# Storing in-place halves as they land, one half by plain copy and GpSimd add, and turns ahead of control and sums

## The reference

```python
g = group_norm(x, groups=32)                     # mean and variance of 16 channels x 3136 pixels
r = relu(g)
r = where(max_pixels(r) - mean_pixels(r) < 0.5, 0, r)        # per channel
bb = 1 - exp(-abs(max_channels(r) - mean_channels(r)))       # per pixel
y = bb * r
pooled = mean_pixels(y)
control = sigmoid(pooled @ W1.T) * where(relu(pooled @ W3.T) < 1, 1.2, relu(pooled @ W3.T))
out = x + where(y < control * max_pixels(y), 0, y)
```

## Time and profile before

| | |
|---|---|
| time, median of 3 runs | 1783.85 us (1779.1 to 1792.09) |
| time of the profiled execution | 1780.24 us |
| its span | 1778.4 us |
| granted PE clock, mean | 0.843 |
| DVE busy | 1460.9 us (82%) |
| ACT busy | 1306.6 us (73%) |
| PE busy, matmul records | 1303.4 us (73%), 19616 |
| PEld busy, records | 1080.2 us (61%), 19616 |
| POOL busy | 610.6 us (34%) |
| HBM read, written | 310.38 MB, 205.52 MB |
| DMA plain queue | 416.38 MB, 58.4% of 16 engines |
| DMA accumulating queue | 99.56 MB, 28.7% of 16 engines |

### The profile page before, as it was taken

How to read it: one execution, slowest core, us unless ns; L and a number is a source line. 1 busy time by engine, 2 the same in 40 slices (tenths; PEclk the granted TensorE clock), 3 DMA queues, 4 the chain that set the end, 5 groups by cost and what they waited for, 6 DMA issues and landing times.

```text
span 1778.4 us, 45243 instructions
## 1 busy us (share of the span) xinstructions
PE 1303.4 (73%) x19616; PEld 1080.2 (61%) x19616; DVE 1460.9 (82%) x2192; ACT 1306.6 (73%) x1921; POOL 610.6 (34%) x446
## 2 busy tenths in 40 slices
PE   4888776788876778767688777678777688777761
PEld 3766655666665666655576655566655566656660
DVE  2588887988887988888888887888887887888987
ACT  5678777777787878777767787777787767777821
POOL 0043233443233444223443233443233442233430
PEclk8898888998888898888888888898878887888885
DMA  9259989999999899998989999989999988899973
GB/s 396 87 162 301 319 315 320 281 296 297 312 330 336 277 285 306 302 329 320 287 263 296 307 330 332 283 277 296 301 330 329 279 265 269 315 329 343 296 228 145
DMA packets 93418, 518.86 MB, mean 292 GB/s; under 512 B 10272, under 2 KB 10272, under 8 KB 93216
## 3 DMA queue, kind: packets, MB, share of 16 engines
q1 hardware_dynamic: 75360, 416.38, 58.4%
q0 software_dynamic: 17856, 99.56, 28.7%
HBM read 310.38 MB, written 205.52 MB: 290 GB/s over the span
## 4 chain that ended last, share of the span: by engine, by line
PE 29%; POOL 26%; ACT 22%; DVE 15%; issue 7%; DMA 1%; SPq 0%; DVEq 0%; ACTq 0%; POOLq 0%
POOL xs L778 23%; ACT rs L476 8%; PE ps_turn L286 7%; PE ps_gate L347 7%; ACT xs L476 7%; PE ps_gate L322 6%; PE ps_gate L294 6%; DVE xs L670 6%; ACT rs L451 5%; DVE rs L670 4%; DVE max_and_mean L622 2%; POOL rstd L757 2%; DMA xs<-in_x 1%; PE ps_gate L356 1%; DVE xs L737 1%
## 5 line engine op out<-in xcount | busy, mean ns | idle before, releaser
L622 DVE TENSOR_REDUCE max_and_mean<-ps_turn 128x2 f32<-128x1024 f32 x384 | 466.0, 1220 | 201.3 <-PE ps_turn L286 200.6
L286 PE MATMUL ps_turn<-ident,xs 128*128 128x128 f32 (+1 forms) x1600 | 358.8, 310 | 177.7 <-DVE max_and_mean L622 112.3
L769 POOL DMA_DIRECT2D xs<-in_x x124 | 111.6, 968 | 940.0 <-DVE xs L670 837.0
L778 POOL TENSOR_TENSOR xs<-xs,rs 128x1568 f32<-128x1568 f32 x124 | 433.3, 3531 | 1.9 <-DVE rs L670 1.9
L286 PEld LDWEIGHTS ps_turn<-ident,xs 128*128 128x128 f32 (+1 forms) x1600 | 204.5, 153 | 311.5 <-DVE max_and_mean L622 155.2
L312 PE MATMUL ps_gate<-ident,bb 128*128 128x128 f32 (+1 forms) x1600 | 273.4, 333 | 153.2 <-ACT bb L469 144.0
L425 ACT ACTIVATE scratch<-xs 128x3136 bf16<-128x3136 f32 x128 | 360.2, 2814 | 7.8 <-DMA xs<-in_x 2.8
L312 PEld LDWEIGHTS ps_gate<-ident,bb 128*128 128x128 f32 (+1 forms) x1600 | 249.6, 239 | 173.4 <-DVE ymax_parts L639 157.7
L286 PE MATMUL ps_turn<-ident,rs 128*128 128x128 f32 (+1 forms) x1600 | 341.3, 299 | 6.0 <-issue 6.0
L639 DVE CUSTOM_DVE_ANT_0 xs<-xs,ps_gate 128x768 f32<-128x768 f32 (+1 forms) x256 | 243.3, 959 | 45.1 <-PE ps_gate L312 45.0
L451 ACT ACTIVATE xs<-xs,shift,rstd 128x3136 f32<-128x3136 f32 x64 | 191.9, 2999 | 100.0 <-POOL shift L761 93.3
(11 more groups left out here) (80 smaller groups left out, 991.9 us busy)
## 6 DMA issues: line engine op xcount, KB each, us to landing
xs<-in_x SPq DMA_DIRECT2D x260, 784.0 KB, 13.7
out<-xs SPq DMA_DIRECT2D x256, 784.0 KB, 8.2
xs<-in_x POOLq DMA_DIRECT2D x124, 784.0 KB, 11.1
rs<-in_L_conv_W SPq DMA_DIRECT2D x2, 1024.0 KB, 18.7
```

Of the source, the lines that this page charges most:

```text
L286: mm = pe.transpose(ps_turn[0:w, n % 2, b - 2 * i, P * t:P * (t + 1)], r_tile(s, t)[:, P * b:P * b + w], ident[:, :])
L622: ins = dve.tensor_reduce(max_and_mean[:, 2 * i:2 * i + 2, 0], ps_turn[:, n % 2, :, :], AX.X, ALU.max)
L778: pool.tensor_tensor(o, o, half(r_tile(s - 1, t), h), ALU.add).then_inc(added, 1)
```

## The change

- SP's order within a round: the stores of tile 0 come first, tile 3's and tile 2's follow as their adds end, and each reload stands closer to the store that it waits for. `LOAD_ORDER`, the order in which loads, squares and sums of x take the tiles, becomes 0, 2, 3, 1.
- Half 0 of tile 1 (`AGAIN`) gets its x otherwise: SP copies it from HBM into `scratch`, once the row means of sample `s + 2` and the logits of sample `s` are made (ACT and PE are done with `scratch`), and POOL adds it as a fifth add. ACT's copy of control rows waits for that add. Three accumulating DMAs a sample remain of four.
- PE: turns 1 and 2 run ahead of all control products, which were interleaved with them; turns 3 and 4 run ahead of the sums of x instead of behind them. The group mean square is two accumulating matmuls instead of one, since the first tile's squares now come as two halves.
- ACT: the first tile of squares is split; its first half stands between the copy of the control rows and the exponential. `copy_group` moves ahead of `gate_values(s, 0)`, and a second `pool_sum` ahead of the last relu.

```diff
--- before.py
+++ after.py
@@ -22,7 +22,8 @@
 XR = 3
 IN_PLACE = (0, 1)
 KEPT_X = (2, 3)
-LOAD_ORDER = (2, 0, 1, 3)
+AGAIN = 1
+LOAD_ORDER = (0, 2, 3, 1)
 RELU_ORDER = (0, 1, 2, 3)
 KEEP_ORDER = (0, 1, 2, 3)
 
@@ -93,7 +94,7 @@
         mean_rows = sb("mean_rows", [P, P])
         ones = sb("ones", [P, 1])
         half_neg = sb("half_neg", [P, T])
-        squares = sb("squares", [P, T])
+        squares = sb("squares", [P, T + 1])
         row_sum = sb("row_sum", [P, 1])
         row_mean = sb("row_mean", [P, T])
         gst = sb("gst", [P, 2, T])
@@ -185,6 +186,8 @@
         exp_neg_ready = sem("exp_neg_ready")
         kept = sem("kept")
         added = sem("added")
+        x_again = sem("x_again")
+        again_added = sem("again_added")
         added_last = sem("added_last")
 
         row_block_cols = row_block[:, :, :].rearrange("p j k -> p (j k)")[:, 0:NBLK]
@@ -223,6 +226,8 @@
             def store(s, t, h):
                 if s == B - 1:
                     sp.wait_ge(added_last, 2 * KEEP_ORDER.index(t) + h + 1)
+                elif t == AGAIN and h == 0:
+                    sp.wait_ge(again_added, s + 1)
                 elif t in IN_PLACE:
                     sp.wait_ge(x_added[s % XR][t][h], 16 * (s // XR + 1))
                 else:
@@ -250,22 +255,26 @@
                     elif nxt == B and t in IN_PLACE:
                         load(B, t, h, src=B - 1)
 
-                store(s, 2, 0)
                 store(s, 0, 0)
                 store(s, 0, 1)
+                reload(0, 0)
+                if s + 2 < B:
+                    sp.wait_ge(row_mean_ready, s + 3)
+                sp.wait_ge(logits_mm, s + 1)
+                sp.dma_start(scratch[:, :], dram_half(x_tiles, s, AGAIN, 0)).then_inc(x_again, 16)
+                reload(0, 1)
+                store(s, 1, 1)
+                store(s, 2, 0)
+                reload(1, 1)
                 store(s, 2, 1)
-                store(s, 1, 0)
-                store(s, 1, 1)
+                store(s, 3, 0)
                 reload(2, 0)
-                store(s, 3, 0)
-                reload(0, 0)
-                reload(0, 1)
                 reload(2, 1)
                 store(s, 3, 1)
+                reload(3, 0)
+                store(s, 1, 0)
+                reload(3, 1)
                 reload(1, 0)
-                reload(1, 1)
-                reload(3, 0)
-                reload(3, 1)
             for t in KEEP_ORDER:
                 for h in range(2):
                     store(B - 1, t, h)
@@ -329,9 +338,12 @@
             def group_stats(s):
                 pe.wait_ge(row_mean_ready, s + 1)
                 pe.matmul(ps_group[:, 0, :], group_pick[:, :], row_mean[:, :], start=True, stop=True)
-                pe.wait_ge(squared, T * (s + 1))
-                pe.matmul(ps_group[:, 1, :], group_avg[:, :], squares[:, :], start=True, stop=True
-                          ).then_inc(group_sums, 1)
+                pe.wait_ge(squared, (T + 1) * (s + 1))
+                first = LOAD_ORDER[0]
+                pe.matmul(ps_group[:, 1, :], group_avg[:, :], squares[:, 0:T], start=True, stop=False,
+                          skip_group_check=True)
+                pe.matmul(ps_group[:, 1, first:first + 1], group_avg[:, :], squares[:, T:T + 1],
+                          start=False, stop=True, skip_group_check=True).then_inc(group_sums, 1)
 
             def count_fails(s):
                 pe.wait_ge(fails_ready, s + 1)
@@ -339,16 +351,15 @@
                     mm = pe.matmul(ps_count, fails[:, t:t + 1], ones[:, :], start=(t == 0), stop=(t == T - 1))
                 mm.then_inc(count_ready, 1)
 
-            def control_products(s, products):
-                for k in products:
+            def control_products(s):
+                for k in range(T):
                     pe.wait_ge(pooled_ready, NS * T * s + T * (NS - 1) + k + 1)
                     for m in range(2):
                         first = 32 * (m + 2 * (k % 2))
                         mm = pe.matmul(ps_control_rows[first:first + NS, :], pooled[:, k, :], wt[:, m, k, :],
                                        start=(k < 2), stop=(k >= T - 2), skip_group_check=True,
                                        tile_position=(0, first))
-                if k == T - 1:
-                    mm.then_inc(control_rows, 1)
+                mm.then_inc(control_rows, 1)
 
             def control_logits(s):
                 pe.wait_ge(control_copied, s + 1)
@@ -377,24 +388,21 @@
             for s in range(B):
                 pe.wait_ge(r_final, s + 1)
                 turn(s, 0)
-                if s > 0:
-                    control_products(s - 1, range(0, 2))
                 turn(s, 1)
-                if s > 0:
-                    control_products(s - 1, range(2, T))
                 turn(s, 2)
                 if s > 0:
+                    control_products(s - 1)
                     control_logits(s - 1)
                 mean_rows_of(s)
                 if s > 0:
                     pe.wait_ge(logits_ready, s)
+                turn(s, 3)
+                turn(s, 4)
                 if s + 1 < B:
                     sum_x(s + 1, range(0, 2))
                 turn_means(s)
                 if s + 1 < B:
                     sum_x(s + 1, range(2, T))
-                turn(s, 3)
-                turn(s, 4)
                 if s + 1 < B:
                     group_stats(s + 1)
                 spread(s, 0)
@@ -411,7 +419,7 @@
                 spread(s, 3)
                 if s + 1 < B:
                     count_fails(s + 1)
-            control_products(B - 1, range(T))
+            control_products(B - 1)
             control_logits(B - 1)
 
         @block.scalar
@@ -419,17 +427,20 @@
             steps = Steps(act, act_step)
             junk_step = Steps(act, squared)
 
-            def square(s, t, cols, part):
-                n = cols.stop - cols.start
+            def square(s, t, cols, at, part):
                 junk_step.wait()
-                ins = act.activation(junk[:, 0:n], x_tile(s, t)[:, cols], ACT.Square, scale=float(HW) ** -0.5,
-                                     accum_out=squares[:, part:part + 1])
-                junk_step.step(ins)
+                junk_step.step(act.activation(junk[:, at], x_tile(s, t)[:, cols], ACT.Square,
+                                              scale=float(HW) ** -0.5, accum_out=squares[:, part:part + 1]))
+
+            def square_half(s, h):
+                t = LOAD_ORDER[0]
+                act.wait_ge(x_loaded[s % XR][t][h], 16 * (s // XR + 1))
+                square(s, t, slice(HALF * h, HALF * (h + 1)), slice(HALF, HW), t if h == 0 else T)
 
             def square_tile(s, n):
                 t = LOAD_ORDER[n]
                 wait_loaded(act, s, t)
-                square(s, t, slice(0, HW), t)
+                square(s, t, slice(0, HW), slice(0, HW), t)
 
             def row_means(s):
                 act.wait_ge(sx_summed, s + 1)
@@ -477,6 +488,8 @@
 
             def copy_control(s):
                 act.wait_ge(control_rows, s + 1)
+                if s > 0:
+                    act.wait_ge(again_added, s)
                 junk_step.wait()
                 act.activation(control_sb, ps_control_rows, ACT.Identity).then_inc(control_copied, 1)
 
@@ -485,7 +498,9 @@
                 act.activation(exp_neg[:, :], logits[:, 0:T], ACT.Exp, scale=-1.0).then_inc(exp_neg_ready, 1)
 
             act.wait_ge(consts_ready, 1)
-            for n in range(T):
+            for h in range(2):
+                square_half(0, h)
+            for n in range(1, T):
                 square_tile(0, n)
             row_means(0)
             copy_group(0)
@@ -497,9 +512,12 @@
                 has_next = s + 1 < B
                 if s > 0:
                     copy_control(s - 1)
+                if has_next:
+                    square_half(s + 1, 0)
+                if s > 0:
                     control_exp(s - 1)
                 if has_next:
-                    square_tile(s + 1, 0)
+                    square_half(s + 1, 1)
                     square_tile(s + 1, 1)
                 copy_mean_rows(s)
                 if has_next:
@@ -508,20 +526,21 @@
                 if has_next:
                     square_tile(s + 1, 3)
                     row_means(s + 1)
+                    copy_group(s + 1)
                 gate_values(s, 0)
                 if has_next:
-                    copy_group(s + 1)
                     relu(s + 1, RELU_ORDER[0])
                 gate_values(s, 1)
                 if has_next:
                     relu(s + 1, RELU_ORDER[1])
                     relu(s + 1, RELU_ORDER[2])
                 gate_values(s, 2)
-                pool_sum(s, 0, 0)
+                for t in range(2):
+                    pool_sum(s, 0, t)
                 if has_next:
                     relu(s + 1, RELU_ORDER[3])
                 gate_values(s, 3)
-                for t in range(1, T):
+                for t in range(2, T):
```

(5 more changed lines are left out.)

## The result

| | before | after |
|---|---|---|
| time, median | 1785.11 us (1779.1 to 1792.09, 4 runs) | 1875.8 us (1872.23 to 1879.78, 4 runs) |
| span of the profiled execution | 1778.4 us | 1876.9 us |
| granted PE clock, mean | 0.843 | 0.820 |
| DVE, ACT, PE busy | 1460.9, 1306.6, 1303.4 us | 1461.3, 1322.6, 1356.1 us |

A forecast was written before the change was run, and what follows sets the result against it. A loop between engines through GpSimd's affine steps and adds, 53.0 us a sample, was taken as the bound. Terms summed to +2.0 us a sample, x 31 = 62, less 1.5: 1841, given as 1842; range 1782 to 1885.

The forecast's parts named there:

- DMA part: Transfers, SP's order and scratch copy: 2 us less DMA a sample, worth nothing in time while DMA has holes.
- The swap: One of four accumulating halves becomes a plain one, 2.0 us of DMA instead of 4.0: worth nothing in time.
- Front: PE's turns 1 and 2 ahead of all control products: -0.3 us a sample, bounds -0.8 and +1.7.
- Middle: PE's turns 3 and 4 ahead of the sums: exposed row sums +0.9 us a sample, spare time at the keep -0.4.
- Stops: PE's waits for instruction loading: all sums of x now lie under accumulates, +1.7 us a sample, bounds 0 and 2.9.
- Behind the group matmul: Gate values 0 behind copy_group delay spread 0, and the early pool sum can delay the relu: +0.3 us a sample.
- DVE "isn't the bound": DVE idles 1.53 us before the first gate, so a later start of POOL's affine steps lengthens the sample.
- Start: In the first sample the first half square needs only half a load: -1.5 us once.
- B: Faster rival: PE's queue gets instruction blocks before it runs dry, -1.7 us a sample, 1726 us; chance 0.08.
- C: Faster rival: DMA was the bound, 2 us a sample go, 1718 us or part of it; chance 0.05.
- E: Scratch copy lands after the four adds, delaying the control copy: up to 3.5 us a sample, 1890 and more; chance 0.05.
- D: PE's instruction stops stay as before, so the 1.7 falls away: 1788 to 1810 us; chance 0.12.

The follow-up runs named there:

- the calm order: Kernel before with scratch copy, fifth add, control-copy wait and the change's LOAD_ORDER, but all stores of finished halves ahead of the reloads: 1786.5 us, 1.0008.
- the three edits: Kernel after with sums of x ahead of turns 3 and 4, gate values 0 ahead of copy_group, second pool sum behind the last relu: 1842.95 us, 1.0355.

## Why the prediction was right in direction and short in size

1875.8 lies 34 us above the forecast, within its range. That agreement is partly luck. The DMA part, worth 59 us alone, stood at 0 in the sum, and stops, which rose by 17 us in all, stood there with 53 (1.7 x 31): the one error nearly covers the other. (From the median 1783.85 and the sum's 61 us the forecast would also have been 1845, not 1842.)

- **DMA part, "worth nothing": wrong, and the largest error.** The swap was rightly put at nothing (the calm order). What failed is the step "the last load still lands some 10 us before its square". The room was 4.5 us on average in before already, not 10; in after it is 4.7 on average, but under 1 us in 8 of 27 samples. The share of 0.17 ahead of the accumulates is that of two microseconds; over the five from 1002 to 1007 it is 0.59. And the step counted transfers and free share of the DMA, not what each reload waits for on SP: the landing of a store that stands right before it in the queue, 9 to 11 us in the chain shown above, one after the other. In the sum it stood at 0; alone it is 59 us, 1.9 us a sample. It also kept a plain half at 2.0 us; with this order of SP it takes 2.2.
- **Front, -0.3 a sample: the mechanism right, the sum short of a term.** The logits do come 0.9 us earlier. Not counted were longer stops of PE, +40.8 us in all, with which the edit costs 1.0 a sample alone in before; why they grow is open. On top of the DMA part it costs nothing, and with GpSimd's transfers held back it moved the time by about -0.5 (not settled), close to the -0.3.
- **Middle, +0.9 - 0.4 = +0.5: right.** The exposed row means are 0.88 us a sample in after and 0.90 in its run alone, which cost 22 us, 0.7 a sample.
- **Stops, +1.7: mis-sized.** They rose by 16.7 us over the run, 0.54 a sample, against a forecast of more than 70 us at sums and turns where 60.7 came. And the reason given, the order of turns and sums, is not the one: that edit alone left them at 46.4. The front (88.1) and SP's order (87.2) raise them.
- **Behind the group matmul, +0.3: the step that DVE "isn't the bound" failed.** It rested on an idle 1.53 us before the gates, a margin that 0.9 us of row mean and a bb later than the group copy use up: the first gate comes 3.2 us later and the adds 0.6. From there DVE's gates set the sample, as the chain shows, and the pool sum waits for gates ahead of the relu. The size was nearly right all the same: the three edits together are worth 33 us, and the sum had 25 for them (0.5 + 0.3 a sample, x 31).
- **Start, -1.5: not seen.** The first sample ended 4.4 us later; it goes through the same orders.

Of the rivals, B (blocks arrive in time) and C (DMA the bound, and so faster) are out. E put a loss on the scratch copy coming late; the fifth add never waited for it in after, and the calm order shows it harmless. D, stops as before, is wrong for the whole change though true of the middle. Of what after would show, PE's idle before the group matmul was right; the last relu at the end of the fourth add was wrong, samples are 56.07 us long, not 55, and stops at sums and turns are 60.7 us, not over 70.

The Trainium skill, Runtime: NRT & Kernel Launch, Instruction fetch mechanics, calls the cost of instruction fetches mostly hidden. For most blocks that holds here: of the 154 of before 30 ended a stop. But PE stood still for 35 to 91 us in these stops, depending on how transfers lay against its densest code, and that is not nothing in a run of 1750 to 1880 us. That a late block queues behind packets of accumulating transfers fits the starts given above and is not proved by them: one block was late with no such packet under way.

**What stays open.** How the cost of SP's order (59 us with the swap, 69 without) divides between late loads and longer stops; both grew together, and no kernel separates them. Why the front raises the stops in before and not on top of the DMA part. What PE's and ACT's orders cost together without SP's order was not run. Nor was holding GpSimd's transfers in before itself, with four of them and no scratch copy.

## What to carry to other kernels

Before a reload is moved nearer to its store in an in-order queue, count the landing time of the store, not only the bytes: a chain of store, wait, reload, store is paid in full latencies, and what is late is the last load of the round. A transfer can be worth delaying on purpose: one wait that kept accumulating transfers off the first half of the densest matmul code gave 1.1%. An edit that costs 1.8% in one kernel can be free in another whose transfers lie differently, so it is worth trying again after they have been moved. And an idle stretch of 1.5 us before an engine is a margin for the sum of all edits on the path to it, to be added up once, not to be spent again by each.

## What the runs showed of the hardware that was not expected

- An accumulating transfer of a half takes 4.1 us of the DMA's time and a plain one by the same queue 2.1.
- Reordering the same packets changed the time that they take from 1549 to 1664 us in all, and all of it in plain stores and loads (2.0 and 2.2 us a half).
- Each of the 546 stops of PE without a releaser, at its sums, turns and means in fourteen traces, ended 1.1 to 1.7 us after a block of instructions had arrived (packet of the instruction queue).
- The landing of a store took 9 to 11 us in a busy stretch (median of all 256: 8.2 in before, 9.6 in after), some five times the 2.0 us of its bytes at 398 GB/s.
- PE's stops at the sums last 0.85 us on average (27 of them) with accumulating transfers held back and 2.5 (18) with them over the sums, in kernels that differ in one wait; in other kernels single ones reached 4.4 us.
- PE's clock fell to the lower of its two levels (1.2 instead of 2.4 GHz) 1.3 us after the end of a stop of 2.19 us and, with gaps of 0.77 and 1.02 us behind it, stayed there for 10.2 us; after a single stop of 2.45 us it was low for 3.4. A spread of 12 matmuls took 2.90 us in the one case and 1.58 in the other. These are two samples; no run changed the gaps alone.
